# First rows of the first batch: statistics by half, weights centred in two places, first keys before the shifts

## The reference

```python
x = x + L0_attn(layernorm(x))    # the change lies at the head of this one
x = x + L0_ffn(layernorm(x))
x = x + L1_attn(layernorm(x))
x = x + L1_ffn(x)

def L0_attn(x):                  # 16 heads of 64, 4 groups of keys and values
    xn = layernorm(x, ln_scale, ln_bias)
    q = xn @ Wq                  # 128 x 1024
    k, v = split(xn @ Wkv)       # 128 x 256 each
    q = layernorm(q, qn_scale, qn_bias)      # over the 64 of a head
    k = layernorm(k, kn_scale, kn_bias)
    attn = softmax(q @ k.T * 64 ** -0.5)     # a group of keys serves 4 heads
    return (attn @ v) @ Wout
```

## Time and profile before

| | us |
|---|---|
| median of 3 runs | 804.23 |
| lowest and highest | 803.65 and 804.3 |
| the profiled execution | 803.57 |
| its span | 801.8 |
| TensorE busy | 770.0 (96%) |
| VectorE busy | 623.8 (78%) |
| GpSimd busy | 591.7 (74%) |
| ScalarE busy | 514.5 (64%) |

### The profile page before, as it was taken

The page is one execution under the profiler, slowest core; times in us unless marked ns, Lnnn a source line. Parts: engine busy times, 40 slices in busy tenths (PEclk is TensorE's granted clock), DMA queues, the critical chain, the costliest instruction groups (busy, mean ns, idle before and its releaser), DMA issues.

```text
span 801.8 us, 21759 instructions
## 1 busy us (share of the span) xinstructions
PE 770.0 (96%) x8750; PEld 522.6 (65%) x8750; DVE 623.8 (78%) x1156; ACT 514.5 (64%) x957; POOL 591.7 (74%) x385
## 2 busy tenths in 40 slices
PE   5998999999999999999899999999999999999988
PEld 5665566666666666676555666666566656988877
DVE  6998788888888777366877788887888877679873
ACT  3875666766676776668656766676677666555522
POOL 2767777888888888946567888788888796455940
PEclk9999999999999999999999999999999999999999
DMA  7000000000000000000000000000000002200001
GB/s 187 5 2 1 2 3 2 2 3 2 2 2 3 2 3 2 2 1 2 1 2 2 2 2 2 2 2 3 3 2 2 3 2 55 58 1 2 1 1 52
DMA packets 50031, 8.57 MB, mean 11 GB/s; under 512 B 42631, under 2 KB 48523, under 8 KB 49931
## 3 DMA queue, kind: packets, MB, share of 16 engines
q1 hardware_dynamic: 49066, 7.05, 5.7%
q10 hardware_dynamic: 864, 0.13, 0.1%
HBM read 5.99 MB, written 1.05 MB: 9 GB/s over the span
## 4 chain that ended last, share of the span: by engine, by line
PE 80%; DVE 10%; issue 3%; ACT 2%; POOL 2%; DMA 1%; SPq 1%; DVEq 0%; ACTq 0%; POOLq 0%
PE psum L742 29%; PE psum L725 21%; PE psum L705 11%; PE psum L771 3%; DVE part L1299 2%; PE psum L591 2%; PE psum L758 2%; PE psum L593 1%; PE psum L592 1%; PE psum L1988 1%; PE psum L1911 1%; PE psum L1958 1%; PE psum L684 1%; ACT space L992 1%; PE psum L1945 1%
## 5 line engine op out<-in xcount | busy, mean ns | idle before, releaser
L560 POOL TENSOR_TENSOR space<-space 128x1024 f32<-128x1024 f32 x160 | 382.7, 2392 | 23.6 <-ACT space L992 5.5
L992 ACT ACTIVATE space<-psum 128x512 f32<-128x512 f32 x512 | 264.0, 604 | 38.2 <-PE psum L725 37.1
L742 PE MATMUL psum<-space,vb 128*32 128x256 f32 x4096 | 247.1, 382 | 2.1 <-ACT space L992 2.1
L1299 DVE TENSOR_REDUCE part<-psum 128x2 f32<-128x1024 f32 x150 | 183.3, 1222 | 32.3 <-PE psum L705 32.3
L742 PEld LDWEIGHTS psum<-space,vb 128*32 128x32 f32 x4096 | 120.9, 110 | 112.1 <-ACT space L992 37.7
L705 PE MATMUL psum<-kh,qh 64*128 64x512 f32 x512 | 117.0, 453 | 6.4 <-DVE part L1299 4.9
L565 POOL TENSOR_TENSOR space<-space 128x1024 f32<-128x1024 f32 x30 | 72.0, 2398 | 67.0 <-DVE space L1317 67.0
L1295 DVE TENSOR_REDUCE part<-psum 128x1 f32<-128x512 f32 x106 | 73.3, 691 | 49.2 <-PE psum L705 46.1
L725 PE MATMUL psum<-qh,kh 64*128 64x512 f32 x512 | 103.2, 396 | 0.1
L725 PE MATMUL psum<-qh,kl 64*128 64x512 f32 x512 | 101.7, 390 | 0.0
L725 PE MATMUL psum<-ql,kh 64*128 64x512 f32 x512 | 101.7, 391 | 0.0
(11 more groups left out here) (265 smaller groups left out, 1102.8 us busy)
## 6 DMA issues: line engine op xcount, KB each, us to landing
ql<-nmx SPq DMA_DIRECT2D x256, 0.5 KB, 2.0
wproj<-in_L_ffn_W SPq DMA_DIRECT2D x4, 256.0 KB, 2.7
out<-x SPq DMA_DIRECT2D x3, 256.0 KB, 2.0
x<-in_L_attn_x SPq DMA_DIRECT2D x2, 256.0 KB, 4.6
wproj<-in_L_attn_Wq SPq DMA_DIRECT2D x1, 512.0 KB, 6.8
x<-in_L_attn_x SPq DMA_DIRECT2D x1, 512.0 KB, 7.7
wout<-in_L_attn_Wout SPq DMA_DIRECT2D x8, 64.0 KB, 4.7
w1s<-in_L_ffn_W SPq DMA_DIRECT2D x2, 256.0 KB, 2.7
```

The costliest lines, as they stand in the source:

```text
L560: pool.tensor_tensor(to, pt[0] if u == 1 else to, pt[u], ALU.add)\
L742: last = pe.matmul(outp[quarter(h, hp), e * QB:(e + 1) * QB], vb[:, place(m)[1], kt, e * QUARTER:(e + 1) * QUARTER], pt[kt][:, h, hp * QB: ...
L992: act.activation(pt[kt][:, h, :], key_scores[kt % 2][h], ACT.Exp).then_inc(exp_made, 1)
L1299: dve.tensor_reduce(to[:, half, :], scores.rearrange("p (h k) -> p h k", h=2), AX_X, ALU.max, negate=True)\
```

## The change

- The variances and the power -0.5 of the first batch are made for 4 tiles at a time (`first_variances`, `first_root`), each half right behind its moments. The count of root_made and var_made grows by one, so the later waits go from b + 2 to b + 3.
- VectorE normalises the first half, then centres the keys' weights (`centre_keys`), then normalises the second half. The products (`crosses`) come after the marks.
- Of the queries' weights VectorE makes the mean only (`mean_queries`); GpSimd subtracts it (`centre_queries`), between the roots and the first twin. cross_made now counts to 2.
- VectorE makes the shifts after the first keys are normalised, not before their sum.
- GpSimd's first twin comes before `scale_first`, not between the two scalings.
- TensorE warms up with 21 transposes instead of 28, and projects the first keys and values before it turns the second half of x; ScalarE squares and keeps them before it keeps that half.

```diff
--- before.py
+++ after.py
@@ -60,7 +60,7 @@
 PAIRED = [0, 2, 1, 3]
 LNS = 4 * CHUNKS
 EARLY = TILES // T
-WARM = 28
+WARM = 21
 
 W_UVB, W_O, W_GATE, W_UP, W_DOWN, W_TILES = 0, 5, 7, 10, 13, 16
 
@@ -463,6 +463,17 @@
                 pool.wait_ge(var_made, count)
                 pool.tensor_tensor(st[:, b, 1, :], st[:, b, 0, :], root_power[:, :], ALU.pow).then_inc(root_made, 1)
 
+            def first_root(half):
+
+                at = slice(half * T, (half + 1) * T)
+                pool.wait_ge(var_made, half + 1)
+                pool.tensor_tensor(st[:, 0, 1, at], st[:, 0, 0, at], root_power[:, at], ALU.pow).then_inc(root_made, 1)
+
+            def centre_queries():
+
+                pool.wait_ge(cross_made, 2)
+                pool.tensor_tensor(centred, centred, over_last(wmean[:, 0:HEADS], DH), ALU.subtract).then_inc(wq_centred, 1)
+
             def scale_first():
 
                 pool.wait_ge(cross_made, 1)
@@ -520,9 +531,11 @@
 
             centred = wproj[:, Q_AT:Q_AT + INNER].rearrange("p (h d) -> p h d", d=DH)
             folded = wproj[:, U_AT:U_AT + INNER].rearrange("p (h d) -> p h d", d=DH)
-            root(0, 1)
+            first_root(0)
+            first_root(1)
+            centre_queries()
+            twin(0, 0)
             scale_first()
-            twin(0, 0)
             scale_rest()
             twin(0, 1)
             take_first()
@@ -564,8 +577,8 @@
                         pool.wait_ge(tail_made, 2 * (n + 1 - b))
                         pool.tensor_tensor(to, to, tail, ALU.add).then_inc(pool_added, 1)
                     if m == SLOTS // 2:
-                        root(1 - b, b + 2)
-                        shift_x(1 - b, b + 2)
+                        root(1 - b, b + 3)
+                        shift_x(1 - b, b + 3)
             pool.wait_ge(shared_in, 16 * len(small))
             pool.wait_ge(exp_made, 2 * TILES * BATCH * SLOTS)
             pool.wait_ge(x_added, SLOTS)
@@ -843,12 +856,12 @@
                 pe.transpose(banks(7, 1)[:, 0:P], ident[:, :], ident[:, :])
             pe.wait_ge(xn_made[0], 1)
             turn_x(0, 0, T)
-            pe.wait_ge(xn_made[0], 2)
-            turn_x(0, T, TILES)
             pe.wait_ge(wk_centred, 1)
             pe.wait_ge(wkv_in, 32)
             pe.wait_ge(xnt_made, 1)
             keys_values(0, 0)
+            pe.wait_ge(xn_made[0], 2)
+            turn_x(0, T, TILES)
             keys_values(0, 1)
             keys_values(0, 2)
             turn_keys(0, 0)
@@ -1083,10 +1096,10 @@
             act.wait_ge(aln_in, 32)
             act.wait_ge(xn_turned, 1)
             keep_x(0, 0, T)
+            square_keys(0, 0)
+            keep_values(0, 0)
             act.wait_ge(xn_turned, 2)
             keep_x(0, T, TILES)
-            square_keys(0, 0)
-            keep_values(0, 0)
             guess_keys(0, 0)
             square_keys(0, 1)
             keep_values(0, 1)
@@ -1197,13 +1210,25 @@
                     last = dve.tensor_scalar(xn[b][:, j, :], x[:, b, j, :], mv[:, j, 0:1], st[:, b, 1, j:j + 1], ALU.subtract, ALU.mult)
                 last.then_inc(xn_made[b], 1)
 
-            def centre(first, heads, made):
-
-                w = wproj[:, first:first + heads * DH].rearrange("p (h d) -> p h d", d=DH)
-                mean = wmean[:, 0:heads]
+            def first_variances(half):
+
+                at = slice(half * T, (half + 1) * T)
+                dve.tensor_scalar(st[:, 0, 0, at], mv[:, at, 1], 1.0 + ATT_EPS, ATT_EPS * LN_EPS, ALU.mult, ALU.add).then_inc(var_made, 1)
+
+            def centre_keys():
+
+                w = wproj[:, K_AT:K_AT + KV].rearrange("p (h d) -> p h d", d=DH)
+                mean = wmean[:, 0:GROUPS]
                 link(dve.tensor_reduce(mean, w, AX_X, ALU.add))
                 link(dve.tensor_scalar(mean, mean, 1.0 / DH, None, ALU.mult))
-                dve.tensor_tensor(w, w, over_last(mean, DH), ALU.subtract).then_inc(made, 1)
+                dve.tensor_tensor(w, w, over_last(mean, DH), ALU.subtract).then_inc(wk_centred, 1)
+
+            def mean_queries():
+
+                w = wproj[:, Q_AT:Q_AT + INNER].rearrange("p (h d) -> p h d", d=DH)
+                mean = wmean[:, 0:HEADS]
+                link(dve.tensor_reduce(mean, w, AX_X, ALU.add))
+                dve.tensor_scalar(mean, mean, 1.0 / DH, None, ALU.mult).then_inc(cross_made, 1)
 
             def crosses():
 
@@ -1488,20 +1513,21 @@
             for h in range(2):
                 dve.wait_ge(x_in[0], 16 * 2)
                 moments(0, h * T, (h + 1) * T)
-            variances(0)
-            crosses()
-            dve.wait_ge(wkv_in, 32)
-            centre(K_AT, GROUPS, wk_centred)
+                first_variances(h)
             dve.wait_ge(root_made, 1)
             normalise(0, 0, T)
+            dve.wait_ge(wkv_in, 32)
+            centre_keys()
+            dve.wait_ge(root_made, 2)
             normalise(0, T, TILES)
             mark_keys()
+            crosses()
             dve.wait_ge(wq_in, 16)
             dve.wait_ge(wk_centred, 1)
-            centre(Q_AT, HEADS, wq_centred)
-            shifts()
+            mean_queries()
             sum_keys(0, 0)
             normal_keys(0, 0)
+            shifts()
             sum_keys(0, 1)
             normal_keys(0, 1)
             sum_keys(0, 2)
```

## The result

The changed kernel takes 806.71 us in the median (805.65 to 807.53, 10 runs), the kernel before, measured again beside it, 804.20 (803.65 to 805.80, 10 runs). The ratio is 1.0025, with a 95% interval of 1.0017 to 1.0032: slower by 2.5 us, where I had forecast 0.3 us less. The time is that of my second rival, 806.6 us, to which I had given a chance of 0.12, and it lies outside my range.

The account below looks back on a forecast made before the run. TensorE, 96% busy, was taken as the bound, with the start of L591's matmul deciding: early leads mostly eaten by the later second twin, 0.3 us gained, 804.23 - 0.3 = 803.9 us; range 802.5 to 805.8.

Parts of the forecast that it names:

- Rival 2: TensorE idle before 24.0: clock falls, the 5.33 us block runs at half rate; 2.4 later, 806.6 us; chance 0.12.
- the sum: All steps up to the matmul of L591 added: it starts at 31.35 instead of 31.69, 0.3 us gained.
- First rows: Start, variances to first transposes: powers 1.02 each, 21 warm-up transposes end near 10.3; x turned at 10.3, 1.8 earlier.
- First keys: First sum of squares at 14.65 instead of 16.97, normalised 16.55, keys turned at 18.0 instead of 20.29: 2.3 earlier.
- Centring on GpSimd: GpSimd centres the queries' weights from 14.15 to 16.05, 1.90, hidden by over 1 us; VectorE loses 1.2 of work.
- The shifts eat the lead: Shifts behind first keys: first scaling at 18.6, second twin done 23.9, second turn 24.0; nothing left of 2.3 us.
- The hole: TensorE idles some 3.2 us in one piece, 20.8 to 24.0, before the second turn of keys; no clock fall priced.
- a rule against it: Trainium skill: an idle TensorE falls back to the halved clock and pays the rise again, turning the gain into loss.
- From there to L591: Second turn to L591: TensorE unbroken to 30.2, queries' copy at 30.27 instead of 30.62, L591 at 31.35 instead of 31.69.
- Rival 3: Start: 21 warm-up transposes too few, first transposes and up to 1.8 us of projection at half rate; 804.8 us; chance 0.12.

Follow-up runs that it names:

- the version with 24 transposes: Changed kernel plus 24 identity transposes on TensorE, filling the 3.4 us idle piece before the second turn of keys: 805.11 us in the median.

## Why the prediction was wrong

Two things went wrong: the fall of the clock behind the hole, which the sum had at nothing (1.58 us), and the lateness of the second turn, which it had too small (0.9 us). By step:

- *First rows.* Right in kind. The powers took 1.04 each (1.02 taken), VectorE was done with the first half at 10.1. The step "with the same rise 21 end near 10.3" was a size taken from one execution: in the profiled one the clock rose only near 11.1, and the first transposes came at 10.82, the first projection at 12.60 instead of 12.0. Where it rose near 9.8 (the version with 24 transposes) they were at 10.22 and 11.87.
- *First keys.* Right: 1.89 from sum to normalised keys (1.87), the 0.6 of delay carried along. First turn at 18.64 (18.0).
- *Centring on GpSimd.* 1.90, as taken, and it hid behind the wait of its own engine. What I missed is that it can stall VectorE; in the changed order only the twin did, by 0.3. From the shift block's start to the first scaling it is 1.78 and not 1.48.
- *The shifts eat the lead.* Right, and mis-sized by those 0.6 and 0.3: second twin done at 24.83 (23.9), second turn at 24.89 (24.0), with the wait put down to GpSimd's twin as forecast.
- *The hole.* **This is the step that failed.** I had it at "some 3.2 us in one piece", had a rule against it, and took the sum without the fall since no row showed one, so the price of the clock stood in it at nothing. The hole was 3.43 us, and in the trace the clock fell at its end; 21 of the 22 executions of this kernel had at least one fall. The argument from the longest hole in the trace (2.0 us at full clock) gave no support for 3.2; it only said nothing. By the Trainium skill (TensorE: Matmul & The Clock Gate, HAM oscillation) an idle engine goes back to half its clock; the trace agrees with 0.51 behind the hole, and the version with 24 transposes shows that it is worth 1.58 us up to the first split matmul.
- *From there to L591.* Right as a mechanism: the copy L971 was held by TensorE's block, not by the folded weights, and the wait shrank from 0.64 to 0.24. With the clock up this stretch took 7.37 (the version with 24 transposes), where the sum has 24.0 to 31.35, 7.35.
- *The rivals.* Rival 2 was the case: middle price 2.7, measured 1.58 of clock; its 806.6 met 806.71 because the lateness that I had not summed (0.94 less 0.37, where I had a gain of 0.3) made up for most of it. That the two meet is luck. Rival 3 was true in part: the first transposes came 0.5 late because the clock rose late, but its sign, projections of over 2 us each, was not seen (1.97 for the first eight matmuls). The chance of 0.12 for the only rival with a page behind it was too low.

What stays open: what pattern of work and idleness makes the clock fall. Traces show one at holes of 3.43 us (21 of 22 executions had a fall somewhere), 2.38 (ten of ten) and 2.10 (8 of 12, falls near the end counted too), and none at one of 2.43 (6 of 11). Open as well is what makes the filled version 1.0 us slower than the kernel before at clock 1.00, and why the kernel before has a fall in about half of its executions; neither was tried.

## What to carry to other kernels

When a step makes one stage early and the next one can't follow, ask what TensorE does between them: an idle piece that is longer than any in the trace can have a cost of its own, the clock, and dummy transposes or a better order are cheap to try. When you move work to GpSimd, look at what VectorE does beside it: one instruction of a group that takes many times the others is the sign that it was held. Compare executions with the same granted clock before calling a microsecond an effect.

## What the runs showed of the hardware

- A VectorE tensor_scalar of 128x63, 0.25 us long, took 1.83 us beside a GpSimd tensor_tensor of 1.90 us, and 0.55 beside a GpSimd tensor_scalar of 0.62; alone it is 0.25 again. VectorE's tensor_scalars of 128x128 (0.34 us) were not held beside a GpSimd power of 1.04, nor a tensor_reduce of 1.21 beside a GpSimd tensor_tensor of 2.37.
- The clock's first rise came between 9.4 and 12.0 us in fourteen traces, by their clock records, with the start of TensorE's work at 6.1 to 6.7 us. The 21 transposes were over at 10.40 where the rise came at 9.80 (24 in the hole), and at 11.03 where it came at 11.09 (the changed kernel).
- A fall can come after work has begun again (0.9 us later). In five traces of the changed order it came 13.65 us after the first rise. One long hole (4.83 us) had 6.8 us at half clock with it, which cost 2.87 us.
